# A transformer block on one core: the feed-forward tiles that run behind the attention pass go one by one, their six TensorE jobs spread over 16 steps, in place of pairs with jobs in consecutive steps

## What is computed

```python
x_proj = silu(x @ W1 + b1)
u, v, q, k = split(x_proj, 4)
attn = silu(einsum('bqhd,bkhd->bhqk', qh, kh)) / S
av = einsum('bhqk,bkhd->bqhd', attn, vh)
y = _layernorm(av * u, gamma, beta) @ W2 + b2
x1 = _layernorm(x + y)
xq = fp4(x1)                                  # w_gate, w_up, w_down are quantised too
h = silu(xq @ w_gate.T) * (xq @ w_up.T)       # 352 wide
out = _layernorm(x1 + fp4(h) @ w_down.T)
```

## Time and profile before

| | |
|---|---|
| runs | 570.9, 570.98, 569.58 us, median 570.9 |
| the profiled execution | 569.8 us, span 567.8 us |
| busy in the span | TensorE 518.6 us (91%), ScalarE 494.6 us (87%), VectorE 183.9 us (32%), POOL 86.6 us (15%) |
| ScalarE's 512 silus of the scores | 478.0 us busy |
| TensorE's score matmuls, its matmuls with v | 179.4 us, 274.8 us busy |
| the chain that ended last | ScalarE 37%, TensorE 28%, VectorE 14%, issue 10%, POOL 9% |

### The profile page before, as it was taken

The page is one execution under the profiler, slowest core; times in us unless marked ns, Lnnn a source line. Parts: engine busy times, 40 slices in busy tenths (PEclk is TensorE's granted clock), DMA queues, the critical chain, the costliest instruction groups (busy, mean ns, idle before and its releaser), DMA issues.

```text
span 567.8 us, 15092 instructions
## 1 busy us (share of the span) xinstructions
PE 518.6 (91%) x6583; PEld 228.4 (40%) x6585; DVE 183.9 (32%) x611; ACT 494.6 (87%) x556; POOL 86.6 (15%) x170
## 2 busy tenths in 40 slices
PE   5699954999999999999999999999999999999996
PEld 2344322334444443434434343434334443444343
DVE  7700097104424340135104420335004510433046
ACT  2599962999999999999999999999999999999910
POOL 6569700002012010110102010200001010201021
PEclk8899995999999999999999999999999999999999
DMA  3312324000000000000000000000000000000000
GB/s 93 111 30 76 109 57 113 1 2 1 3 10 2 2 6 8 1 2 2 12 1 3 1 10 2 1 3 2 12 1 1 2 10 3 2 2 10 2 0 11
DMA packets 11960, 10.24 MB, mean 18 GB/s; under 512 B 1939, under 2 KB 11414, under 8 KB 11894
## 3 DMA queue, kind: packets, MB, share of 16 engines
q1 hardware_dynamic: 10998, 7.87, 5.0%
q0 software_dynamic: 896, 1.40, 0.9%
HBM read 1.92 MB, written 1.05 MB: 5 GB/s over the span
## 4 chain that ended last, share of the span: by engine, by line
ACT 37%; PE 28%; DVE 14%; issue 10%; POOL 9%; DMA 1%; DVEq 0%; POOLq 0%
ACT attn L571 36%; PE ps L360 25%; POOL q_stack L287 2%; POOL rstd_a L354 2%; POOL rstd_b L354 1%; PE ps L505 1%; POOL k_stack L287 1%; DVE w_qk L817 1%; DVE amax_a L696 1%; DVE xn_a L706 1%; DVE xn_a L705 1%; DVE xn_a L699 1%; DVE feat L666 1%; POOL ve_a L353 1%; DVE mv_a L729 1%
## 5 line engine op out<-in xcount | busy, mean ns | idle before, releaser
L571 ACT ACTIVATE attn<-ps 128x1024 f32<-128x1024 f32 x512 | 478.0, 1140 | 36.2 <-PE ps L360 35.6
L360 PE MATMUL ps<-attn,v_pad 128*32 128x256 f32 x4096 | 274.8, 386 | 0.5 <-ACT attn L571 0.5
L360 PE MATMUL ps<-q_stack,k_stack 64*128 64x256 bf16 x2048 | 179.4, 274 | 17.7 <-issue 3.2
L360 PEld LDWEIGHTS ps<-attn,v_pad 128*32 128x32 f32 x4096 | 107.1, 109 | 99.2 <-issue 53.2
L360 PEld LDWEIGHTS ps<-q_stack,k_stack 64*128 64x128 bf16 x2048 | 67.4, 94 | 159.9 <-ACT attn L571 117.7
L353 POOL TENSOR_TENSOR ve_a<-mv_a,eps_col 128x1 f32<-128x1 f32 x24 | 4.6, 190 | 458.8 <-DVE mv_a L729 458.8
L723 DVE SCALAR_TENSOR_TENSOR zu<-ps,uT 128x256 f32<-128x256 f32 x8 | 3.4, 425 | 124.1 <-PE ps L360 124.1
L727 DVE BATCH_NORM_STATS2 stats_a<-ps 128x6 f32<-128x128 f32 x8 | 2.4, 299 | 58.6 <-PE ps L360 58.6
L360 PE MATMUL ps<-zeros 128*128 128x512 bf16 x76 | 19.1, 405 | 1.4 <-DVE zeros L804 1.2
L779 DVE TENSOR_TENSOR gate_a<-gate_a,ps 128x352 f32<-128x352 f32 x7 | 3.6, 521 | 50.6 <-PE ps L360 50.6
L360 PE MATMUL ps<-wgate_t,xqT 128*128 128x352 f32 x32 | 13.4, 505 | 1.8 <-ACT gate_a L571 1.8
(11 more groups left out here) (156 smaller groups left out, 356.9 us busy)
## 6 DMA issues: line engine op xcount, KB each, us to landing
k_stack<-parts SPq DMA_DIRECT2D x48, 64.0 KB, 2.1
q_stack<-parts SPq DMA_DIRECT2D x18, 128.0 KB, 2.4
x_sb<-in_L_attn_x SPq DMA_DIRECT2D x4, 256.0 KB, 5.4
q_stack<-parts POOLq DMA_DIRECT2D x12, 64.0 KB, 2.3
out<-x_a SPq DMA_DIRECT2D x8, 64.0 KB, 1.5
out<-x_b SPq DMA_DIRECT2D x8, 64.0 KB, 1.6
w_sb<-in_L_attn_W SPq DMA_DIRECT2D x1, 256.0 KB, 3.2
wdown_n<-in_L_ffn_w_down POOLq DMA_DIRECT2D x1, 176.0 KB, 2.5
```

Of the source, the lines that this page charges most:

```text
L360: return pe.matmul(to, lhsT, rhs, start=start, stop=stop, skip_group_check=True)
L571: return act.activation(to, frm, ACT.Silu, **kw)
```

## The change

The pair table goes, and each of the tiles 0 to 13 gets a base step and six offsets of its own. Line numbers of the kernel after are 5 to 7 higher.

```diff
-    PAIR_BASE = [45, 68, 100, 132, 164, 196, 228]
-    PAIR_JOBS = {0: ("y", 0), 5: ("xqT", 0), 6: ("gate", 0), 7: ("gate", 1), 8: ("up", 0), 9: ("up", 1),
-                 14: ("hqT", 0), 15: ("hqT", 1), 16: ("down", 0)}
+    TAIL = KT - 2
+    TILE_AT = {t: (BEGIN[t // 2 + 1] + LAG + 16 * (t % 2), {"y": 0, "xqT": 5, "gate": 7, "up": 9, "hqT": 13, "down": 15})
+               for t in range(TAIL)}
+    TILE_AT[TAIL - 2] = (BEGIN[TAIL // 2] + LAG, {"y": 0, "xqT": 4, "gate": 6, "up": 8, "hqT": 12, "down": 13})
+    TILE_AT[TAIL - 1] = (len(STEPS) - 16, {"y": 0, "xqT": 5, "gate": 7, "up": 9, "hqT": 13, "down": 15})
...
+            for tile in range(TAIL):
                 for which in range(3):
-                    for r in ROWS:
...
+                    rstd(ROWS[tile % 2], which)
...
                 if kind == "y":
-                    y_of(2 * p, bank, 0)
-                    return y_of(2 * p + 1, bank, 2 * P)
+                    return y_of(tile, bank, 0)
                 if kind == "xqT":
-                    pe.wait_ge(xq_ready, 2 * p + 2)
...
+                    pe.wait_ge(xq_ready, tile + 1)
+                    return pe.transpose(ps[:, bank, 0:P], r.xn[:, 0:D], ident[:, :])
...
-                down_of(ROWS[0], bank, 0)
-                return down_of(ROWS[1], bank, P)
+                return down_of(r, bank, 0)
...
+            def to_out(tile):
+                r = ROWS[tile % 2]
+                bank = wait_made("down", 0, tile)
+                dve.tensor_tensor(r.x1p[:, :], ps[:, bank, 0:D], r.x1[:, :], ALU.add).then_inc(job_by_vec, 1)
+                wait_taken("down", 0, tile)
+                statistics(r.x1p[:, :], 2, r)
+                finish(tile)
```

More of the change, by code:

```diff
@@ L96, in build, with chunk_of @@
     job_no = {job: k for k, job in enumerate(JOBS)}
-    ACT_JOBS = [k for k, (kind, i, p) in enumerate(JOBS)
-                if kind in ("k", "q", "v", "u") or (kind == "gate" and p is not None)]
+    ACT_JOBS = [k for k, (kind, i, tile) in enumerate(JOBS)
+                if kind in ("k", "q", "v", "u") or (kind == "gate" and tile is not None)]
     VEC_JOBS = [k for k in range(len(JOBS)) if k not in ACT_JOBS]
[L100 to L104, removed]
+    def chunk_of(tile):
+        return max(c for c in range(len(WIDTHS)) if Q0[c] <= tile * P)
     with ExitStack() as ctx:
@@ L348, in _, with rstd @@
             var_no = Count()
-            for p in range(LAST + 1):
-                for which in range(3):
-                    for r in ROWS:
[L352 to L355, removed]
+            def rstd(r, which):
+                pool.wait_ge(var_ready, var_no.next())
+                link(pool.tensor_tensor(r.ve[:, :], r.mv[:, which, 1:2], eps_col[:, :], ALU.add))
+                pool.tensor_tensor(r.rstd[:, which:which + 1], r.ve[:, :], minus_half[:, :],
+                                   ALU.pow).then_inc(rstd_ready, 1)
+            for tile in range(TAIL):
+                for which in range(3):
+                    rstd(ROWS[tile % 2], which)
+            for which in range(3):
+                for r in ROWS:
+                    rstd(r, which)
         @block.tensor
@@ L462, in job @@
             def job(at):
-                kind, i, p = JOB_AT[at]
-                k = job_no[(kind, i, p)]
+                kind, i, tile = JOB_AT[at]
+                k = job_no[(kind, i, tile)]
                 bank = JOB_BANK[k]
@@ L472, in job @@
                     pe.wait_ge(av_taken, STEPS[at - LAG][0])
-                if p is not None:
-                    last = behind(kind, i, p, bank)
+                if tile is not None:
+                    last = behind(kind, tile, bank)
                 elif kind in ("u", "q", "k"):
@@ L496, in y_of @@
             def y_of(tile, small, off):
-                c = pair_chunk(tile // 2)
+                c = chunk_of(tile)
                 z = zu[:, tile * P - Q0[c]:(tile + 1) * P - Q0[c]]
@@ L512, in down_of, with behind @@
                 return last
[L514 removed]
+            def behind(kind, tile, bank):
+                r = ROWS[tile % 2]
                 if kind == "y":
[L516 to L517 removed]
+                    return y_of(tile, bank, 0)
                 if kind == "xqT":
[L519 to L521 removed]
+                    pe.wait_ge(xq_ready, tile + 1)
+                    return pe.transpose(ps[:, bank, 0:P], r.xn[:, 0:D], ident[:, :])
                 if kind == "gate":
[L523 removed]
+                    return mm(ps[:, bank, 0:FF], xqT[:, tile % 2, :], wgate_t[:, :])
                 if kind == "up":
[L525 removed]
+                    return mm(ps[:, bank, 0:FF], xqT[:, tile % 2, :], wup_t[:, :])
                 if kind == "hqT":
[L527 to L530 removed]
+                    pe.wait_ge(hq_ready, tile + 1)
+                    return hqT_of(r, bank)
+                return down_of(r, bank, 0)
             for at in range(len(STEPS)):
@@ L606, in job @@
                 act.wait_ge(job_made, k + 1)
-                if p is None:
+                if tile is None:
                     project(kind, i, JOB_BANK[k]).then_inc(job_by_act, 1)
                 else:
-                    silu(ROWS[i].gate[:, :], ps[:, JOB_BANK[k], 0:FF]).then_inc(job_by_act, 1)
+                    silu(ROWS[tile % 2].gate[:, :], ps[:, JOB_BANK[k], 0:FF]).then_inc(job_by_act, 1)
             for at in range(len(STEPS)):
@@ L643, in link, with wait_made, wait_taken @@
                 dve.wait_ge(vec_order, order.next())
[L645 to L647 removed]
+            def wait_made(kind, i, tile):
+                k = job_no[(kind, i, tile)]
                 dve.wait_ge(job_made, k + 1)
                 return JOB_BANK[k]
[L651 to L652 removed]
+            def wait_taken(kind, i, tile):
+                dve.wait_ge(job_by_vec, VEC_JOBS.index(job_no[(kind, i, tile)]) + 1)
             def split(kind, c):
@@ L719, in take_av @@
                 dve.wait_ge(av_done, BEGIN[c + 1])
-                for p in range(LAST):
-                    if pair_chunk(p) == c - 1:
-                        dve.wait_ge(job_made, job_no[("y", 0, p)] + 1)
+                for tile in range(TAIL):
+                    if chunk_of(tile) == c - 1:
+                        dve.wait_ge(job_made, job_no[("y", 0, tile)] + 1)
                 dve.scalar_tensor_tensor(out=zu[:, 0:w], in0=ps[:, AV[c], 0:w], scalar=1.0 / S,
@@ L738, in y_plus_x, with quantised_x @@
                                                 in1=x_sb[:, tile, :], op0=ALU.mult, op1=ALU.add)
-            def quantised_x():
+            def quantised_x(rows):
                 tensors = []
-                for r in ROWS:
+                for r in rows:
                     dve.wait_ge(rstd_ready, rstd_no.next())
@@ L747, in quantised_x, with quantised_h @@
                 fp4(tensors, xq_ready)
-            def quantised_h():
+            def quantised_h(rows):
                 fp4([Blocks(r.gate[:, :].rearrange("p (b k) -> p b k", k=BLOCK),
[L751 to L781, removed]
@@ L783, in copy_hqT @@
-            def copy_hqT(p):
-                fn = FT[2][1]
[L785 to L798, removed]
+                            r.xn[:, :].rearrange("p (b k) -> p b k", k=BLOCK), P, NBF, r) for r in rows], hq_ready)
@@ new lines, in finish, with to_quantised_x @@
+            def finish(tile):
+                r = ROWS[tile % 2]
+                dve.wait_ge(rstd_ready, rstd_no.next())
+                if tile >= 2:
+                    dve.wait_ge(out_written[tile % 2], 16 * (tile // 2))
+                normalise(r.x1p[:, :], r.x2[:, :], 2, r).then_inc(x2_ready, 1)
+            def to_quantised_x(tile):
+                r = ROWS[tile % 2]
+                bank = wait_made("y", 0, tile)
+                statistics(ps[:, bank, 0:P], 0, r)
+                y_plus_x(r, ps[:, bank, P:2 * P], tile).then_inc(job_by_vec, 1)
+                wait_taken("y", 0, tile)
+                statistics(r.x1p[:, :], 1, r)
+                quantised_x([r])
@@ new lines, in copy_xqT, with to_quantised_h @@
+            def copy_xqT(tile):
+                bank = wait_made("xqT", 0, tile)
+                dve.tensor_copy(xqT[:, tile % 2, :], ps[:, bank, 0:P]).then_inc(job_by_vec, 1)
+            def to_quantised_h(tile):
+                r = ROWS[tile % 2]
+                bank = wait_made("up", 0, tile)
+                dve.wait_ge(job_by_act, ACT_JOBS.index(job_no[("gate", 0, tile)]) + 1)
+                dve.tensor_tensor(r.gate[:, :], r.gate[:, :], ps[:, bank, 0:FF], ALU.mult).then_inc(job_by_vec, 1)
+                wait_taken("up", 0, tile)
+                quantised_h([r])
@@ new lines, in copy_hqT @@
+            def copy_hqT(tile):
+                r = ROWS[tile % 2]
+                fn = FT[2][1]
+                bank = wait_made("hqT", 0, tile)
+                dve.tensor_copy(r.hqT[:, 0:2, :].rearrange("p t n -> p (t n)"), ps[:, bank, 0:2 * P])
+                dve.tensor_copy(r.hqT[0:fn, 2, :], ps[0:fn, bank, 2 * P:3 * P]).then_inc(job_by_vec, 1)
+            def to_out(tile):
```

(19 more changed lines are left out.)

16 lines of the change are left out of this document (8 added, 8 removed).

## The result

The median fell from 570.9 to 561.5 us (four runs, 560.5 to 562.9); the ratio is 0.984 with a 95% interval from 0.981 to 0.987. The forecast was 559.0, with 552 to 566 as its range, so the direction held, and the gain came out smaller, 9.5 us (1.6%) instead of 11.9 (2.1%) against the median of before.

A forecast was written before the change was run, and what follows sets the result against it. ScalarE's silu rate, 0.917 us each, was taken to set the pace, with TensorE feeding it scores. The terms summed as 569.8 - 19.7 + 7.7 + 0.6 + 0.2 + 0.4 = 559.0 us, range 552 to 566.

The forecast's parts named there:

- The five breaks of a pair period: ScalarE pauses waiting for scores, from jobs in consecutive steps; 2.82 us per pair, at best 19.7 us go.
- The wait for zu at six boundaries: Even tile's y job, one step behind the odd tile's down, waits for VectorE; 1.28 us each, 7.7 us added.
- The chain itself: VectorE and POOL work from down's end through x1p, statistics, normalisation and zu until TensorE sees it; 2.74 us.
- down at 15: One tile's down job at offset 15, priced 0.77 us, would find 0.83 of TensorE lead and leave 0.06.
- the 0.04 that they were to leave: Gate and up, 0.79 us each on TensorE, would each leave 0.04 of a 0.83 us lead, not stopping ScalarE.
- full reserve: The most TensorE can be ahead of ScalarE through three pairs of score banks; taken as 0.83 us.
- odd tiles' y: Odd tile's y job, one step after a down, would lose 0.08 us, seven times, 0.6 in all.
- tiles 12 and 13: Tile 12's down right behind hqT loses 0.12 us, its neighbour's y 0.06 more; 0.2 us added.
- last multiplication and zu: Last down job in step 255 delays the final multiplication with v and the zu behind it; 0.4 us added.
- the spaced jobs would break the run: Rival, 14%: gate, up, down and y each overdraw TensorE's lead and stop ScalarE; 7 us more, 566.
- VectorE's single-tile chain: Rival, 3%: VectorE's one-tile work is late at xqT, needing 10 us instead of 6.2; 570 us or more.
- A slower ScalarE: Rival, 4%: silus end further apart than 0.917 us once ScalarE hardly stops; at 0.946, 571 to 572 us.

The follow-up runs named there:

- down_at_14: Changed kernel with jobs of tiles 0 to 11 at offsets 0, 4, 6, 8, 12, 14, one step without a job between down and y; 552.2 us.
- up_behind_gate: Changed kernel with the up job in the step right behind gate (offset 8; 7 for tile 12), nothing else moved; 567.5 us.
- pairs_spread: Kernel before, tiles still in pairs, with jobs spread to offsets 0, 5, 6, 8, 10, 12, 18, 20, 22; 560.2 us.
- zu_first: Changed kernel with take_av of a finished chunk moved ahead of the odd tile's to_out on VectorE; 555.0 us.
- longer_chain: Changed kernel with two extra, unread VectorE additions between to_out and take_av for odd tiles 1 to 11; 571.8 us.
- gate_twice: Changed kernel with the gate matmul of every job tile done twice into the same bank, output the same; 568.9 us.

## Why the prediction was right, and what was mis-sized

**The pace.** ScalarE's ends set it, 0.917 us per silu and 0.355 per gate. All versions show this rate, down_at_14 with 0.918 over 256 silus and chunks only 0.07 above the 59.38 that ScalarE needs, which is 0.04 for each of two down jobs.

**What goes.** The five breaks of a pair period are gone, as forecast. up_behind_gate brings the one at gate and up back at its old price, and pairs_spread shows that spacing does it with pairs too.

**What comes.** The wait for zu at six boundaries was the largest new term. It was forecast at 1.28 each and costs 1.36. The chain itself was right to the last digit: the y job starts 295.38 - 292.64 = 2.74 behind down. zu_first takes the wait away and longer_chain lengthens it by what is put in, so this cause is shown, not argued.

**The mis-sized term: what a job for one tile costs.** The prediction took "down at 15 (half of 1.53, 0.77)" and for y "about half of 0.82, I take 0.43". TensorE's rows of the changed kernel, with the gate job and an odd tile's y:

```profile
307.83 0.86 PE L367 MATMUL ps<-wgate_t,xqT 128*128 128x352 f32 x2
...
308.62 0.61 PE L367 MATMUL ps<-q_stack,k_stack 64*128 64x256 bf16 x8
...
311.71 0.86 PE L367 MATMUL ps<-wup_t,xqT 128*128 128x352 f32 x2
...
324.26 1.07 PE L367 MATMUL ps<-attn,v_pad 128*32 128x256 f32 x16
...
325.27 0.33 PE L507 MATMUL ps<-ident,zu 128*128 128x128 f32 x1
```

Down takes 292.64 - 291.77 = 0.87. The y job takes 0.48: 325.75, the next scores, less 325.27. Half a job costs more than half: 2 x 0.87 - 1.53 = 0.21 and 2 x 0.48 - 0.82 = 0.14 more for two jobs than for one. gate_twice shows a fixed part of the same size from the other side, 0.79 for the first multiplication and 0.59 for one more: about 0.2 us of a job does not grow with its work. What this part is made of is not shown. Gate and up always were jobs of one tile, so their 0.79 needed no halving, and the 0.04 that they were to leave held. So down on a full reserve loses 0.04 where 0.06 should have been left, and an odd tile's y, down included, loses 0.22 instead of 0.08. At the six boundaries, too, most of the difference to the forecast is this 0.10.

| us | forecast | measured |
|---|---|---|
| breaks that go, 7 pairs | -19.7 | -19.9 (62.22 - 59.38 = 2.84 each) |
| six boundaries | 7.7 | 8.4 (1.36 + 0.04 each) |
| odd tiles' y | 0.6 | 1.3 (six of 0.22) |
| tiles 12 and 13 | 0.2 | 0.4 |
| last multiplication and zu | 0.4 | 0.5 |
| sum | -10.8 | -9.3, as the pass shows |

The last row but one is the way from the last scores to zu: 4.39 before (537.57 to 541.96), 4.68 after, plus 0.19 that the smaller reserve is worth. So 1.5 of the 2.5 us between forecast and median are in the sum, nearly all of it the price of a job for one tile. What is left, about 1 us, is the base: I started from the profiled execution of before, 569.8, which lies 1.1 below the median of the runs.

**The rivals.** That the spaced jobs would break the run did not happen: gate and up lose nothing. VectorE's single-tile chain is not late. A slower ScalarE is out by down_at_14.

## What to carry to other kernels

Where one engine sets the pace and another feeds it through a few buffers, treat the lead of the feeder as a small account: measure how much it can hold, what a step earns and what each job takes, and look for the job that overdraws it. Spread work so that none does. Then look at what the spreading has put back to back: the producer of a job's input may stand in its engine's queue behind work that was finished long before in the old order, and moving it ahead may cost nothing, as in zu_first. Do not halve the price of a job when you halve the job.

## What was unexpected in the hardware

- At four of the six boundaries of longer_chain, TensorE's granted clock fell around the end of a wait of 2.3 us (to 0.63 over the next two steps in the place shown), and about 1 us was lost on top of the wait. At three of the four it fell behind the wait. At the one near 360 us it had fallen already when the wait ended: the transpose of zu takes 0.45 us there instead of 0.30. A wait of 1.1 us did this at none of the 18 boundaries of the changed kernel, up_behind_gate and gate_twice.
- In the profiled execution after, the clock in the head (0.54 against 0.83 in the same stretch) went with a pass that starts 2.6 us later, with the same program up to there. The other traces put the pass's start in the order of this clock too. The four runs of the changed kernel differ by about that much (2.4 us).
- In an unbroken run silus start 0.903 us apart but end 0.917 apart, so their durations grow along the run, and a break first pays that lead back. Losses must be counted from ends. Two places of one run in the kernel before, ten silus apart, two silus each (start, length):

```profile
227.54 2.19 ACT L571 ACTIVATE attn<-ps 128x1024 f32<-128x1024 f32 x2
...
236.57 2.32 ACT L571 ACTIVATE attn<-ps 128x1024 f32<-128x1024 f32 x2
```

(236.57 - 227.54) / 10 = 0.903 from start to start, and (236.57 + 2.32 - 227.54 - 2.19) / 10 = 0.916 from end to end.
